# A recommender's pairwise dots: two more features looked up with one-hot matmuls, two samples' dots at once in half of TensorE's columns, dots stored in long runs

## What is computed

```python
e = stack([tbl_f[ids[:, f]] for f in range(26)], axis=1)     # 2048 x 26 x 128
combined = concatenate([dense[:, None, :], e], axis=1)       # 2048 x 27 x 128
dots = einsum('bfd,bgd->bfg', combined, combined)[:, IU0, IU1]   # 351 pairs
h = concatenate([dense, dots, dense], axis=1)                # 607
h = maximum(h @ W_top1 + b_top1, 0)                          # 512
h = maximum(h @ W_top2 + b_top2, 0)                          # 256
y = h @ W_top3
```

## Time and profile before

| | us |
|---|---|
| median of 3 runs (lowest, highest) | 410.31 (408.68, 413.03) |
| the profiled execution, whole | 410.8 |
| its span, first to last instruction | 409.0 |
| PE busy (share) | 377.0 (92%) |
| mean granted PE clock | 0.982 |
| DMA | 63.03 MB, 64119 packets, mean 154 GB/s |

### The profile page before, as it was taken

One profiled execution on the slowest core, in us unless ns is written; L12 is line 12 of the kernel. 1 busy time (PEld: TensorE's weight loads), 2 busy tenths in 40 slices (PEclk: granted clock), 3 DMA queues, 4 the chain that ended last, 5 costly groups with the idle time before them and its releaser, 6 DMA issues.

```text
span 409.0 us, 6187 instructions
## 1 busy us (share of the span) xinstructions
PE 377.0 (92%) x2288; PEld 307.5 (75%) x2288; DVE 263.9 (65%) x422; ACT 207.5 (51%) x302; POOL 274.1 (67%) x264
## 2 busy tenths in 40 slices
PE   0895988789979989999999999999999999999996
PEld 0684768579958886787969697787869694859986
DVE  3998899699499786994985766985895010101132
ACT  2241457528573664473837474574828364846400
POOL 6887887777777777777777777777777757700000
PEclk9998999989997999999999999999999999999999
DMA  7984889846975698669385894669353731454400
GB/s 186 273 242 119 230 232 231 243 116 133 216 226 135 138 205 209 198 126 220 92 217 146 189 217 138 189 131 211 93 150 72 161 93 45 91 109 50 73 20 1
DMA packets 64119, 63.03 MB, mean 154 GB/s; under 512 B 46008, under 2 KB 47701, under 8 KB 64089
## 3 DMA queue, kind: packets, MB, share of 16 engines
q1 hardware_dynamic: 53626, 45.52, 47.0%
q0 software_dynamic: 8192, 16.79, 15.9%
q10 hardware_dynamic: 2270, 0.33, 0.5%
HBM read 54.08 MB, written 8.53 MB: 153 GB/s over the span
## 4 chain that ended last, share of the span: by engine, by line
PE 84%; POOL 6%; DMA 4%; issue 3%; DVE 2%; SPq 1%; ACT 1%; DVEq 0%; ACTq 0%
PE look_bank L509 33%; PE short_bank L582 22%; PE out_bank L542 20%; PE short_bank L565 6%; POOL rows L475 6%; DMA bias<-in_b_top 2%; PE out_bank L553 2%; DVE one_hot L751 1%; DMA rows<-in_tbl,all_ids 1%; DMA all_ids<-in_ids 1%; ACT looked_up L619 0%; DVE hidden L771 0%; DVE low_table L732 0%; DVE combined L762 0%; SPq L395 0%
## 5 line engine op out<-in xcount | busy, mean ns | idle before, releaser
L475 POOL DMA_INDIRECT rows<-in_tbl,all_ids x256 | 273.2, 1067 | 82.3 <-issue 77.1
L751 DVE TENSOR_TENSOR one_hot<-spread_ids,chunk_row 128x512 fp32r<-128x512 int32 x246 | 154.4, 695 | 27.7 <-DMA spread_ids<-in_ids_by_feature 19.9
L509 PE MATMUL look_bank<-one_hot,high_table 125*128 125x512 f32 x328 | 152.8, 466 | 20.6 <-DVE low_table L732 16.3
L509 PE MATMUL look_bank<-one_hot,low_table 125*128 125x512 f32 x328 | 132.6, 404 | 0.0
L582 PEld LDWEIGHTS short_bank<-combined 128*108 128x108 f32 x1024 | 99.6, 175 | 6.4 <-issue 5.3
L582 PE MATMUL short_bank<-combined 128*108 128x108 f32 x1024 | 100.0, 258 | 2.7 <-ACT combined L637 2.7
L509 PEld LDWEIGHTS look_bank<-one_hot,high_table 125*128 125x128 f32 x328 | 64.5, 197 | 46.1 <-issue 20.7
L509 PEld LDWEIGHTS look_bank<-one_hot,low_table 125*128 125x128 f32 x328 | 64.6, 197 | 22.3 <-issue 10.6
L665 ACT COPY dots<-short_bank 108x432 f32<-108x432 f32 x128 | 65.2, 521 | 28.8 <-PE short_bank L582 28.4
L619 ACT COPY looked_up<-look_bank 128x512 f32<-128x512 f32 x40 | 23.5, 588 | 100.8 <-PE look_bank L509 100.7
L762 DVE COPY combined<-short_bank 128x512 f32<-128x512 f32 x32 | 21.8, 690 | 67.5 <-PE short_bank L565 67.3
(11 more groups left out here) (18 smaller groups left out, 76.4 us busy)
## 6 DMA issues: line engine op xcount, KB each, us to landing
whole_table<-in_tbl SPq DMA_DIRECT2D x36, 448.0 KB
spread_ids<-in_ids_by_feature SPq DMA_DIRECT2D x40, 256.0 KB, 4.8
block_scratch<-dots SPq DMA_DIRECT2D x24, 208.0 KB, 3.8
rows<-in_tbl,all_ids POOLq DMA_INDIRECT x256, 4.0
whole_table<-in_tbl SPq DMA_DIRECT2D x4, 560.0 KB
pairs<-block_scratch SPq DMA_DIRECT2D x9, 234.0 KB
whole_table<-in_tbl SPq DMA_DIRECT2D x36, 52.0 KB
block_scratch<-dots SPq DMA_DIRECT2D x24, 52.0 KB, 3.4
```

The source lines that it names most:

```text
L475: nc.gpsimd.indirect_dma_start(rows[:, t % 2, slot, :], None, tables[ROW_FEATURES[slot]][:, :], bass.IndirectOffsetOnAxis(ap=all_ids[:, t, ...
L509: last = nc.tensor.matmul(look_bank[s % LOOK_BANKS][:], table_parts[part][s % TABLE_PLACES][0:ROWS_K, c, :], one_hot[0:ROWS_K, (chunks_bef ...
L751: last = nc.vector.tensor_tensor(to, of, row.to_broadcast([P, COLS]), ALU.is_equal)
```

## The change

Tables 2 and 4 (1250 rows, ten chunks each) are looked up and no longer gathered: 12 and 14 features, a block then has nine tables of eight chunks and three of ten, and six halves follow each tile. Gathered features form groups of 4, 4, 4 and 2.

The dots are made for two samples at once: 54 moving columns, and as weights 59 columns (the 54 and five more, so that 32 rows can be stored from row 27). The first two samples of a group of four write to partitions 0 to 58, the other two to partitions 64 to 122 of the same bank. A bank takes eight groups of four samples (432 values a partition), so that a tile fills the four banks once, and no dots wait for an earlier bank of the same tile. ScalarE makes four copies of 128 partitions a tile. Each tile's first use of the banks is by transposes (before tile 0 two transposes of the identity fill up the last group).

`dots` becomes `all_dots`, laid out for each half block so that all columns of one row and all groups lie together: a store's run is 26 x 64 x 4 = 6,656 bytes (and 13 x 64 x 4 = 3,328 in the second store, which now has 32 rows in place of 16). There are two scratch tensors in DRAM for half blocks. The pairs are loaded by half and by sample j of the group of four: 12 DMAs a half in runs of 256 bytes, 24 a block in place of 3. SP issues the first half's loads ahead of the second half's stores, and the second half's where the loads of the unit stood. After the last tile SP and ACT share stores and loads by sample.

In the last block, the first two products of a unit come ahead of the third layer of the unit before it.

```diff
-LOOKED_UP = {0: 1250, 1: 1000, 5: 1000, 7: 1000, 9: 1000, 17: 1000, 20: 1000, 22: 1000, 24: 1000, 25: 1000}
+LOOKED_UP = {0: 1250, 1: 1000, 5: 1000, 7: 1000, 9: 1000, 17: 1000, 20: 1000, 22: 1000, 24: 1000, 25: 1000,
+             2: 1250, 4: 1250}
...
-LOOK_PLACES = 15
+LOOK_PLACES = 18
...
-N_GROUPS = N_ROW // IN_GROUP
+N_GROUPS = -(-N_ROW // IN_GROUP)
+GROUP_ROWS = [min(IN_GROUP, N_ROW - g * IN_GROUP) for g in range(N_GROUPS)]
...
-PER_BANK = 4
+
+AT_ONCE = 2
+SQUARE = AT_ONCE * VECTORS
+HALF_P = P // AT_ONCE
+SPAN = P // IN_QUAD
+LOADED = VECTORS + SPAN
+PER_BANK = 8
 FILLS = QUADS // PER_BANK
-SQUARE = IN_QUAD * VECTORS
...
-HALVES_AFTER = [6, 5, 5, 4]
+HALVES_AFTER = [6, 6, 6, 6]
...
     if m == LAST:
-        half = out_steps(LAST)
+        half, one, two = out_steps(LAST), out_steps(LAST + 1), out_steps(LAST + 2)
+
         return [out_steps(LAST - 1)[:12], out_steps(LAST - 1)[12:-1], half[:6],
-                half[6:] + out_steps(LAST + 1) + out_steps(LAST + 2)][u]
+                half[6:-1] + one[:2] + half[-1:] + one[2:-1] + two[:2] + one[-1:] + two[2:]][u]
...
+        def store_dots(h, j):
+
+            to, of = scratch_of(h)[j * SPAN:(j + 1) * SPAN], dots_of(h)
+            row, c = j // AT_ONCE * HALF_P + j % AT_ONCE * VECTORS, j % AT_ONCE * VECTORS
+            return [(to[:, 1:VECTORS, :], of[row:row + SPAN, c + 1:c + VECTORS, :]),
+                    (to[:, VECTORS:WRAPPED, :], of[row:row + SPAN, c:c + REACH, :])]
+
+        def load_pairs(v, h, k, j):
+
+            first, tiles = STORED[h]
+            u = first - UNITS[v][0] * PER_BLOCK - UNITS[v][1] // P
+            to = pairs[0:K_PAIRS, k, UNITS[v][1]:UNITS[v][2]].rearrange("p (j q) -> p j q", j=IN_QUAD)
+            step = WRAPPED + 1
+            at = step * F_PER_K * k + 1
+            of = scratch_of(h)[j * SPAN:(j + 1) * SPAN].rearrange("f g q -> (f g) q")[at:at + step * F_PER_K]
+            of = of.rearrange("(f k) q -> f k q", k=step)[:, 0:REACH]
+            return to[:, j, u * QUADS:(u + tiles) * QUADS], of
...
-            def load_unit(v, slices):
-                sp.wait_ge(*stored(v))
+            def load_part(h, samples):
+                v = unit_of(STORED[h][0])[0]
+                sp.wait_ge(*part_stored(h))
                 if v > 0:
 
                     sp.wait_ge(out_done, out_number(UNITS[v][0] - 1, LAYER1))
-                for k in slices:
-                    to, of = load_pairs(v, k)
-                    sp.dma_start(to, of).then_inc(loaded(v)[0], 16)
+                for j in samples:
+                    for k in range(PAIR_SLICES):
+                        to, of = load_pairs(v, h, k, j)
+                        sp.dma_start(to, of).then_inc(loaded(v)[0], 16)
...
-                for h, part in enumerate(STORED):
-                    if t + 1 == sum(part):
-
-                        store_part(h, range(IN_QUAD // 2) if last else range(IN_QUAD))
+                ends = [h for h, part in enumerate(STORED) if t + 1 == sum(part)]
+                for h in ends:
+                    if h % 2 == 1 and h < 2 * LAST:
+                        load_part(h - 1, range(IN_QUAD))
+
+                    store_part(h, range(IN_QUAD // 2) if last else range(IN_QUAD))
                 for s in looks[:1]:
                     load_ahead(s)
-                v, place = unit_of(t)
-                if place == unit_tiles(v) - 1:
-                    load_unit(v, range(0, PAIR_SLICES, 2) if last else range(PAIR_SLICES))
+                for h in ends:
+                    if h % 2 == 1 or h >= 2 * LAST:
+                        load_part(h, range(IN_QUAD // 2) if last else range(IN_QUAD))
                 for s in looks[1:]:
                     load_ahead(s)
...
             def turn_group(t, g):
-                if t > 0:
+                if t > 0 and g >= N_GROUPS - FILLS:
 
                     pe.wait_ge(dots_copied, t * FILLS - N_GROUPS + g + 1)
...
                 for b in range(FILLS):
-                    if b >= SHORT_BANKS:
-
-                        pe.wait_ge(dots_copied, t * FILLS + b - SHORT_BANKS + 1)
                     for q in range(PER_BANK):
-                        quad = b * PER_BANK + q
-                        of = combined[:, quad * IN_QUAD:(quad + 1) * IN_QUAD, :].rearrange("d j v -> d (j v)")
-                        last = nc.tensor.matmul(short_use(t, N_GROUPS + b)[0:SQUARE, q * SQUARE:(q + 1) * SQUARE], of, of,
-                                                start=True, stop=True)
+                        for j in range(0, IN_QUAD, AT_ONCE):
+                            at = ((b * PER_BANK + q) * IN_QUAD + j) * VECTORS
+                            row = j // AT_ONCE * HALF_P
+                            last = nc.tensor.matmul(fill_bank(b)[row:row + LOADED, q * SQUARE:(q + 1) * SQUARE],
+                                                    all_combined[:, at:at + LOADED], all_combined[:, at:at + SQUARE],
+                                                    start=True, stop=True)
                     last.then_inc(dots_done, 1)
...
-                nc.scalar.copy(dots[0:SQUARE, :, at:at + PER_BANK],
-                               short_use(t, N_GROUPS + b)[0:SQUARE, 0:PER_BANK * SQUARE].rearrange(
-                                   "p (q c) -> p c q", q=PER_BANK)).then_inc(dots_copied, 1)
+                nc.scalar.copy(dots_of(h)[:, :, at:at + PER_BANK],
+                               fill_bank(b)[:, 0:PER_BANK * SQUARE].rearrange("p (q c) -> p c q", q=PER_BANK)).then_inc(
+                                   dots_copied, 1)
```

More of the change, by code:

```diff
@@ L190, in out_number, with part_of, unit_parts @@
     return v * OUTS + i
+def part_of(t):
+    h = next(h for h, (first, tiles) in enumerate(STORED) if first <= t < first + tiles)
+    return h, t - STORED[h][0]
+def unit_parts(v):
+    return [h for h, (first, _) in enumerate(STORED) if unit_of(first)[0] == v]
 def unit_of(t):
@@ L295, in build @@
         late_copied = sem("late_copied")
-        scratch_stored = [sem(f"scratch_stored{i}") for i in range(4)]
+        scratch_stored = [sem(f"scratch_stored{i}") for i in range(5)]
         pairs_loaded = [sem(f"pairs_loaded{i}") for i in range(4)]
@@ L314, in landed @@
         def landed(t, g):
-            return gathered[t % 2][g], (t // 2 + 1) * 16 * IN_GROUP
+            return gathered[t % 2][g], (t // 2 + 1) * 16 * GROUP_ROWS[g]
         def part_stored(h):
             if h < 2 * LAST:
[L321 to L326, removed]
+                return scratch_stored[h % 2], STORES * 16 * (h // 2 + 1)
@@ L328, in loaded, with dots_of @@
+            return scratch_stored[2 + h - 2 * LAST], STORES * 16
         def loaded(v):
[L330 removed]
+            return pairs_loaded[max(0, v - LAST + 1)], PAIR_LOADS * len(unit_parts(v)) * 16 * (v + 1 if v < LAST else 1)
         def copied(n):
             return (out_copied, n + 1) if n < LAST * OUTS else (late_copied, n + 1 - LAST * OUTS)
+        def dots_of(h):
+            first, tiles = STORED[h]
+            at = first % PER_HALF * SQUARE * QUADS
+            return all_dots[:, at:at + SQUARE * tiles * QUADS].rearrange("p (c q) -> p c q", c=SQUARE)
@@ new lines, in scratch_of @@
+        def scratch_of(h):
+            return block_scratch[h % 2] if h < 2 * LAST else last_scratch[h - 2 * LAST]
+        def store_dots(h, j):
[4 more added lines that the diff above has]
+        def load_pairs(v, h, k, j):
+            first, tiles = STORED[h]
+            u = first - UNITS[v][0] * PER_BLOCK - UNITS[v][1] // P
[5 more added lines that the diff above has]
+            return to[:, j, u * QUADS:(u + tiles) * QUADS], of
@@ L350, in result_and_place @@
                     out_bank[out_number(v, THIRD) % OUT_BANKS][:, a // P:b // P])
[L352 to L374, removed]
         @block.sync
@@ L557, in turn_group @@
             def turn_group(t, g):
-                if t > 0:
+                if t > 0 and g >= N_GROUPS - FILLS:
                     pe.wait_ge(dots_copied, t * FILLS - N_GROUPS + g + 1)
-                elif g == 0:
-                    pe.wait_ge(constants_ready, 1 + len(chunk_row))
+                if t == 0 and g == 0:
+                    pe.wait_ge(constants_ready, 2 + len(chunk_row))
                 pe.wait_ge(*landed(t, g))
-                for q in range(IN_GROUP):
-                    last = nc.tensor.transpose(short_use(t, g)[:, q * P:(q + 1) * P], rows[:, t % 2, g * IN_GROUP + q, :],
+                for q in range(GROUP_ROWS[g]):
+                    last = nc.tensor.transpose(short_bank[g][:, q * P:(q + 1) * P], rows[:, t % 2, g * IN_GROUP + q, :],
                                                identity[:])
+                for q in range(GROUP_ROWS[g], IN_GROUP if t == 0 else 0):
+                    last = nc.tensor.transpose(short_bank[g][:, q * P:(q + 1) * P], identity[:], identity[:])
                 last.then_inc(turned_done, 1)
@@ L718, in _ @@
                     nc.scalar.dma_start(to, of).then_inc(part_stored(h)[0], 16)
```

(11 more changed lines are left out.)

33 lines of the change are left out of this document (16 added, 17 removed).

## The result

The changed kernel takes 429.24 us (median of 4 runs, 426.18 to 432.31), the kernel before 410.11 beside it: ratio 1.0457, interval 1.0361 to 1.0554. The prediction said 406.5, with 399 to 428 as its range, and a small gain where there is a loss. The profiled execution has a span of 426.5 (409.0 before).

What follows compares the result with a forecast made beforehand. It took PE to bound the kernel from tile 4 on, VectorE before. Tile 4's dots at 160.1, tile 12's at 334.6, a last block of 69.4 and 1 for the clock gave span 405.0, median 406.5 us; range 399 to 428.

Steps and rivals of the forecast that it cites:

- the rival of queued loads: Dots: weight loads of the two halves queue up, 6.3 us a tile, time 443; chance 0.15.
- The term: Dots of a tile: halves side by side, 64 x 50 ns = 3.2 us in place of 6.08, -2.9.
- the sum: Whole kernel: stage times added along the engine that is late, to a span of 405.0 us.
- both sums, 71.5 and 160.1: Start and block 0, VectorE setting the pace: tile 0's dots start at 71.5 us, tile 4's at 160.1.
- the sum had 1, added at the end: Before tile 4's dots: PE's clock loss after a gap costs 0 to 3 us, counted as 1.
- 24 x 0.4 = 9.6. SP's sum is level: SP's queue: 24 pair loads of 0.4 us a block, eight stores 3.2; about 16 a block before and after.
- it costs nothing: Ids behind SP's last 12 loads: 5 us late once a block, VectorE 5 ahead; at worst 5 a block.
- Rival (c): Blocks 1 and 2: VectorE also bounds, ids late by 5 us each time; up to 10 more, 407 to 417; chance 0.05.
- The sign given for it: Trace sign of late ids: VectorE waits for ids of over 5 us with PE waiting behind.
- I counted it for tile 4 (1.8): Ahead of tile 4's dots: the copies after the block's last look take 1.8 us.
- 69.4: Last block: 81.6 us now, less 4 x 2.9 for dots, less 0.7 for six transposes.
- the balance of a steady block, +8.3 against -11.5: PE's steady block: 91.4 + 9.2 looking-up - 0.9 transposes - 11.5 dots = 88.1 us.

Runs made afterwards that it cites:

- a_ids4: The changed kernel with four places for the spread ids in place of three, all loads kept in SP's queue: 421.33 us, ratio to the kernel before 1.0244.

## Why the prediction was wrong

- *The dots.* Right in kind: the halves run side by side, and the rival of queued loads is refuted by 3.61 beside the 7.07 of one half. The term was too small: 3.61 and not 3.2 a tile, a pair of pairs 56 ns and not 50. With fourteen transposes at 1.68 in place of 1.53 (I had scaled 1.75 by 14/16) and looks at 0.2315 in place of 0.23 each, a quiet tile is 0.65 longer than the sum, 5 us over blocks 1 and 2, 2 in the last block. The 0.83 ns a column that I called the transposes' is the third layer's; by the earlier trace rows theirs is 0.85, which changes little.
- *Start and block 0.* Right that VectorE sets the pace there: both sums, 71.5 and 160.1, stand within 2 us. In part this is luck. VectorE's last table of the block is ready at 153.6 (forecast 153.7), but it started tile 0's one-hots at 83.8 and not 85.7, and waited 2.0 for ids, which the sum did not have. The 2 us are in PE's 20 matmuls behind the gap, 6.42 in place of 4.6; of this the sum had 1, added at the end.
- *SP's queue.* This is the step that failed: "24 x 0.4 = 9.6. SP's sum is level" and "it costs nothing". A load takes about 0.8 us of issue, and the row that I had on record says so: 2.46 for three. I took the 0.4 of a table load for it. The loads take 18.8 to 19.2 us a block and not 9.6, eight stores 4.9 to 5.7 and not 3.2, so SP's sum is about 30 a block and not 16. The ids behind it come late by more than VectorE's lead: it waits 7.0 and 3.6 us around tile 8 where I had allowed 5 and a lead of 5, and 4.9 and 3.0 around tile 4, where by my own sum VectorE set the pace and had no lead. Gaps of 0.6, 1.6, 2.2 and 1.7 us in tiles 4 and 8 are 6.2 of the 17.4; taking the cause away gives 7 to 8.6 (a_ids4) in blocks 1 and 2. Rival (c) named it, at 0.05 and "up to 10": right mechanism, chance far too low. The sign given for it, waits for ids of over 5 us with PE waiting behind, is what the trace shows.
- *Moves.* No step had the copy and move of the block's last look in blocks 1 and 2; I counted it for tile 4 (1.8) and not for tiles 8 and 12: 1.1 each.
- *Stops inside the dots.* The dots of tile 4 take 4.8 us (162.07 to 166.90) and those of tile 11 5.2 (328.01 to 333.19) in place of 3.61: 2.8 in blocks 1 and 2, more in block 0 where VectorE covers it. The sum had no such term.
- These sum up to 5.3 + 6.2 + 2.2 + 2.8, and the third layer's 0.2, 16.7 of the 17.4. The rest is about what the first four matmuls behind each of the four gaps lose, at 0.29 us each in place of 0.23.
- *Last block.* 72.5 for 69.4: 2 from the dots and transposes, 0.2 from a third layer, and PE's waits behind tile 15's dots sum up to 2.5 in place of 2.1, 0.6 of them for loads of the last pairs. Some 0.4 stays open.
- *Which part does what.* The sum had the answer and I didn't ask it. It puts tile 4's dots 14.7 later, where VectorE sets the pace and faster dots are no help, and gives the features 8.3 (9.2 - 0.9) more in each of blocks 1 and 2: 31.3 by tile 12. Between the runs with ten and twelve it is 41.1 by tile 12 (354.0 - 312.9; 7 to 8.6 of it are SP's queue, and 6.8 that tile 4's dots start earlier with ten than before the change), and 32.6 at the end. I looked only at the balance of a steady block, +8.3 against -11.5, as though the features were a part of the gain. In the steady blocks they cost nothing by the sum: with ten, GpSimd's gathers make blocks 1 and 2 174.3 long, and the forecast for twelve was 174.5. By the sum the price is paid ahead of tile 4. Measured against ten it is 23.5 there (9.8 and 13.7) and 17.6 in blocks 1 and 2.

## What to carry to other kernels

Price a DMA's issue by the row of that very DMA, and multiply it before anything else: here its bytes said nothing of it (loads of 234 KB and of 29 KB each take SP about 0.8 us). Then ask what stands behind it in the same queue, and give what stands there one more buffer. Where two engines share a work, the split is decided over start, middle and end: a share that is level in the steady part can lose 10 us ahead of it, where nothing covers it. And a change of several parts is worth running part by part: this one was 4% of gain and 8 to 9% of loss.

## What was not expected of the hardware

- Two matmuls of 54 columns in the two halves of the array start 28 ns apart (3.61 us for 128), in one half 55 ns (7.07). This is close to the least distance of about 25 ns between the starts of small matmuls that the Trainium skill gives (TensorE: Matmul & The Clock Gate, Wait — 56ns, not 53.3ns?); no run here shows whether 28 is that floor or half of 55.
- PE can stop inside a run of small matmuls, waiting for nothing that the profile shows. In the changed kernel PE stops inside the dots of tile 4 after 102 of 128 instructions, for 0.88 us (chain above); with three loads a half it stops at the same place for 2.25, with four places for ids for 0.34. In the kernel before, and when all dots are in one half and take 7.07, no dots are broken off on these chips; with ten features and 3.61 a tile none are either, so small matmuls alone don't do it. On the other chip the dots of 7.07 are broken off as well, for 95 us in all. PE running out of instructions would fit stops without a semaphore, but no run here tests it, and the cause stays open.
- GpSimd's gathers took as long in sum with 224 as with 256 (271.2 and 273.2 us): 1.21 us each in place of 1.07. Why, no run here shows.
